# Cross-attention and FP4 FFN on one core: start of the first block, the pair loop of its weight phase, and the softmax between blocks in another order

## Chip, cores and metric

The kernel runs on one NeuronCore of a Trainium2 chip. The metric is device time in microseconds (us). PE is TensorE (matmuls), ACT is ScalarE, DVE is VectorE, POOL is GpSimd, SP is SyncE, which here only issues DMAs.

## What is computed

Two layers on x (2 x 2048 rows of 512): a cross attention over 77 text tokens whose scores are additive, then an FFN whose operands are quantised blockwise to FP4.

```python
f = layernorm(x)                                          # 4096 rows in all, d = 512
h = tanh((ctx @ Ws)[:, None] + (f @ W)[:, :, None] + b)   # per row, per token, per feature
rho = (h @ w) + mask;  att = softmax(rho)                 # 77 scores per row
txt = att @ ctx
x = x + tanh(txt @ Wcw) * f + tanh(txt @ Wcb)
n = layernorm(x)
gate, y = q4(n) @ q4(w_gate).T, q4(n) @ q4(w_up).T        # w_gate, w_up: 1408 x 512
x = x + q4(silu(gate) * y) @ q4(w_down).T                 # q4: blocks of 16 to FP4 and back
```

The tanh over rows x tokens x features is the largest piece: 4096 * 77 * 512 values.

## The kernel before

The 4096 rows are 32 tiles of 128, in four **blocks** of 1024 rows. Of one block the scores are made in 77 **quads** (QPB). A quad is four ACT instructions of 128x1024 (`tanh_quad`, L438: one feature chunk `e`, four tokens), each into one of four places of half of the ring `hring`, and 16 PE matmuls as the profile counts them (`score_quad`, L548) that reduce them with `w` into `rho`. The ring holds two quads: ACT may write quad n when PE has used quad n - 2 (`quad_used`). Engines run their instructions in written order, and all sync is by semaphores, so the order in each engine's program is the schedule.

**Head** (before the first quad). DVE normalises the 8 tiles of block 0 in two halves of 4 (`rows_head`), PE turns them (`turn_head`), ACT copies them out (`copy_head`), PE makes the text projection (L517) and the eight feature projections (`project_head`, chunk e, half hh), DVE copies each into `featT` (L749). Then PE makes `uv` (L532). Only then does it come to `score_quad(0)`.

**Block 0** carries two other loads between its quads. The remaining 24 tiles are normalised and projected as 12 **pairs**: DVE `rows_pair(w)` (L754 to L736), PE `turn_pair(w)` (L563), DVE `copy_pair(w)` (L762), PE `project_pair(w, 0)` and `(w, 1)` (L575), DVE `features_pair(w)` (L773). And DVE quantises the FFN weights: 11 times a piece of gate and one of up (`gate_up_weights`, 128x512 each, L694 to L717), then 4 pieces of down (`down_weights`, 128x1408). One loop on DVE holds both. On PE, pair w is turned after quad `at(w)`, and `project_pair(w - 1, ...)` follows quads `at(w) + 1` and `at(w) + 2`, so behind `turn_pair(w)`.

**FFN tiles.** From tile t = 0 on, each tile has seven steps on PE: `gate_up(t, 0..3)` (L611) and `down(t - 1, 0..2)` (L623). The quads of the next block are spread over these steps by cost in the table `slots`. ACT makes `silu_tanh` (L458) after step 0 to 3's quads plus two; DVE makes `hidden` (L908, L909), `rows_tile(t + 1)` and `quantise_hidden(t)` (L694 to L717 at 128x1408). Scoring of block k ends in step (t, 2) of t = 6, 14, 22 (`SOFTMAX_AT`), and there the **block change** lies: `softmax_drain` (DVE L847, frees `rho`), `softmax_transposes` of two halves (PE L599), `softmax_shift` of two halves (DVE L854, L855), `softmax_exp` (ACT), `softmax_sums` (DVE), `softmax_gates` (ACT), `softmax_factors` (DVE), which tile t + 2 needs.

```python
for w in range(NC + KC):           # DVE, block 0
    ...
    if w < PAIRS:
        copy_pair(w)
    if 0 < w <= PAIRS:
        features_pair(w - 1)
    if w + 1 < PAIRS:
        rows_pair(w + 1)
```

Of the kernel before, what the change touches and what calls it, by code (L numbers as in the profile page):

```python
# [29 lines left out]
def bass_xattn_fp4_ffn(nc, x, ctx_in, mask_in, Ws_in, W_in, w_in, b_in, Wcw_in, bcw_in, Wcb_in, bcb_in,  # L30
# [29 lines left out]
    def quad_at(q):  # L60
        if q < 2 * KC:
            return q % 2, q // 2
        return q // KC, q % KC
# [16 lines left out]
    for k in range(1, NBLK):  # L80
        t0, p0 = (0, 0) if k == 1 else (BASE[k - 1] - 2, 5)
# [25 lines left out]
    with ctx:  # L107
# [6 lines left out]
        def sem(name):  # L114
# [75 lines left out]
                     [rho[:, 0:512], rho[:, 512:1024], tr[:, :], dn[:, :]]]  # L190

# [25 lines left out]
        text_filled = sem("text_filled")  # L217
        bias_ready = sem("bias_ready")
# [31 lines left out]
        FEAT = [(0, 0), (1, 0), (0, 1), (1, 1), (2, 0), (2, 1), (3, 0), (3, 1)]  # L250

        def feat_at(e):
            return max(i for i, (ee, _) in enumerate(FEAT) if ee == e) + 1

# [4 lines left out]
        def _(sp):  # L259
# [8 lines left out]
            sp.dma_start(Wf, W_in.rearrange("(k p) e -> p k e", p=P)).then_inc(loaded_w, 16)  # L268

# [18 lines left out]
            load_gu(1, 0)  # L288
            sp.wait_ge(head_turned, 2)
# [95 lines left out]
        def _(act):  # L385
            act.dma_start(ctx_nat[0:TOK], ctx_in.rearrange("b t d -> t b d")).then_inc(loaded_ctx, 16)
            for n, src in enumerate((w_in, b_in, Wcw_in, Wcb_in)):
                flat = src.rearrange("a b -> (a b)")
                act.dma_start(cols[:, n, :], flat.rearrange("(k p) -> p k", p=P),
                              allow_slow_non_contiguous=True).then_inc(loaded_c, 16)  # L390
            act.dma_start(Wsf, Ws_in.rearrange("(k p) e -> p k e", p=P)).then_inc(loaded_ws, 16)
            for n, src in enumerate((bcw_in, bcb_in)):
                act.dma_start(bc[:, n:n + 1], src.rearrange("(a n) -> a n", a=1).broadcast_to([P, 1])).then_inc(loaded_c, 16)
            act.wait_ge(mask_filled, 1)
            for g in range(GRP):
                act.dma_start(mask_i[SLOTW * g:SLOTW * g + FULLR, :],
                              mask_in[:, 0:GRP * FULLR].rearrange("b (i g) -> i b g", g=GRP)[:, :, g],
                              allow_slow_non_contiguous=True).then_inc(loaded_m, 16)
            act.dma_start(mask_i[FULLR:FULLR + 1, :], mask_in[:, TOK - 1:TOK].rearrange("b t -> t b"),
                          allow_slow_non_contiguous=True).then_inc(loaded_m, 16)  # L400
# [17 lines left out]
            for e in range(KC):  # L418
                act.wait_ge(text_filled, e // 2 + 1)
                act.activation(bias[:, e, :], gu[0][e // 2][:, (e % 2) * BATCH * TOK:(e % 2 + 1) * BATCH * TOK],  # L420
                               ACT.Identity, bias=cols[:, 1, e:e + 1]).then_inc(bias_ready, 1)
            copy_head(1)
            act.wait_ge(bias_ready, KC)

            def tanh_quad(n):
# [5 lines left out]
                if k == 0 and q < 2 * KC and q % 2 == 0:  # L431
                    act.wait_ge(feat_ready, feat_at(q // 2))
# [50 lines left out]
        def _(pe):  # L483
# [16 lines left out]
            def project_head(i):  # L500
                e, hh = FEAT[i]
                pe.wait_ge(xnT_ready, 4 * hh + 4)
                again = [j for j in range(i) if FEAT[j][0] % 2 == e % 2 and FEAT[j][1] == hh]
                if again:
                    pe.wait_ge(feat_ready, again[-1] + 1)
                for k in range(KC):
                    last = pe.matmul(gu[e % 2][hh][:, :], Wf[:, k, e * P:e * P + P], xnT4[hh][:, k, :],
                                     start=(k == 0), stop=(k == KC - 1))
                last.then_inc(feat_filled, 1)

# [3 lines left out]
            for e in range(KC):  # L514
                o = (e % 2) * BATCH * TOK
                for k in range(KC):
                    last = pe.matmul(gu[0][e // 2][:, o:o + BATCH * TOK], Wsf[:, k, e * P:e * P + P], ctxT[:, k, :],  # L517
                                     start=(k == 0), stop=(k == KC - 1))
                if e % 2:
                    last.then_inc(text_filled, 1)  # L520
            pe.wait_ge(loaded_w, 16)
            pe.wait_ge(bias_ready, KC)
            project_head(0)
            project_head(1)
            turn_head(1)
            for i in range(2, len(FEAT)):
                project_head(i)
            pe.wait_ge(wcol_ready, 1)
            for u in range(2):
                o = u * BATCH * TOK  # L530
                for k in range(KC):
                    last = pe.matmul(tr[:, o:o + BATCH * TOK], wcol[:, u, k, :], ctxT[:, k, :],  # L532
                                     start=(k == 0), stop=(k == KC - 1))
            last.then_inc(uv_filled, 1)
# [19 lines left out]
            def turn_pair(p):  # L554

                pe.wait_ge(xn_ready, HEAD_T + 2 * p + 2)
                if p == 0:
                    pe.wait_ge(uv_ready, 1)
                else:
                    pe.wait_ge(pair_copied, p)  # L560
# [416 lines left out]
```

## Time and profile before

| | |
|---|---|
| median of 3 runs | 1740.33 us (1736.83 to 1742.61) |
| profiled execution | 1740.98 us, span 1739.2 us |
| busy share of the span | PE 85%, ACT 77%, DVE 67% |
| ACT busy | 1347.2 us, of it tanh of the quads 1293.0 us |
| mean granted clock of PE | 0.957 |

The span falls in three parts. To 42 us the head runs; to about 1441 us ACT makes tanh (first beside the pairs, then beside the FFN tiles 0 to 22); from there nine more tiles follow in which DVE is busy nearly all the time. The profile marks in brackets how long an engine sat idle before an instruction, and what released it.

### The profile page before, as it was taken

To read this page: it belongs to the slowest core of one execution; us is meant where nothing else is said; L and a number is where in the kernel's file an instruction comes from. 1 tells how busy PE (TensorE), PEld (TensorE's weight loads), DVE (VectorE), ACT (ScalarE), POOL (GpSimd) and SP (SyncE) were. 2 spreads that over 40 slices of the span, in tenths; PEclk is the share of its full clock that TensorE was granted. 3 is DMA by queue.
4 is the path that set the end of the run, shared out by engine and by line. 5 is a ranking of instruction groups with operands and counts; after the bars stand their busy time and mean duration, and the time that the engine had idled before them with its cause. 6 is when DMAs were issued, how large, how long until landed. Compare 5 with 4: busy or idle time off the path is not lost.

```text
span 1739.2 us, 23935 instructions
## 1 busy us (share of the span) xinstructions
PE 1482.2 (85%) x9752; PEld 651.5 (37%) x9752; DVE 1169.9 (67%) x2111; ACT 1347.2 (77%) x1391; POOL 2.7 (0%) x18
## 2 busy tenths in 40 slices
PE   6788888765888899889999999899999998689886
PEld 4234444311333333333333333333333334345442
DVE  4579999864475435467655555676555557999994
ACT  2798898899999999969999999699999992000000
POOL 0000000000000000000000000000000000000000
PEclk9999999888999999999999999999999999899997
DMA  3123332330011111211211111102211111122212
GB/s 129 37 62 75 74 75 63 76 73 15 13 24 35 35 35 24 36 35 16 55 36 36 36 36 35 36 13 59 35 36 36 35 36 36 37 54 62 58 41 51
DMA packets 180754, 77.88 MB, mean 45 GB/s; under 512 B 163851, under 2 KB 163851, under 8 KB 180645
## 3 DMA queue, kind: packets, MB, share of 16 engines
q1 hardware_dynamic: 177392, 74.99, 19.0%
q10 hardware_dynamic: 3253, 1.37, 0.3%
q8 instruction: 76, 1.25, 0.3%
q14 instruction: 33, 0.27, 0.1%
HBM read 27.85 MB, written 8.39 MB: 21 GB/s over the span
## 4 chain that ended last, share of the span: by engine, by line
ACT 56%; DVE 29%; PE 11%; issue 2%; ACTq 1%; DMA 1%; DVEq 0%; SPq 0%
ACT hring L438 54%; DVE work L703 4%; PE rho L548 3%; DVE work L714 2%; DVE work L715 2%; DVE sm L694 2%; ACT th L458 2%; DVE work L909 1%; DVE work L908 1%; DVE sm L697 1%; DVE work L713 1%; DVE work L712 1%; PE dn L623 1%; DVE work L716 1%; DVE work L717 1%
## 5 line engine op out<-in xcount | busy, mean ns | idle before, releaser
L438 ACT ACTIVATE hring<-featT,bias 128x1024 f32<-128x1024 f32 x1232 | 1293.0, 1140 | 80.9 <-PE rho L548 76.2
L548 PE MATMUL rho<-hring,wslide 128*32 128x512 f32 x4928 | 614.9, 623 | 136.7 <-ACT hring L438 136.7
L548 PEld LDWEIGHTS rho<-hring,wslide 128*32 128x32 f32 x4928 | 133.5, 112 | 499.9 <-ACT hring L438 271.7
L623 PE MATMUL dn<-wd_room,turned 128*128 128x512 f16 x1056 | 243.7, 383 | 13.4 <-DMA turned<-work 13.4
L908 DVE SCALAR_TENSOR_TENSOR work<-th,gu1g 128x352 f32<-128x352 f32 x64 | 33.3, 521 | 266.6 <-ACT th L458 265.9
L611 PE MATMUL gu0g<-wg,turned 128*128 128x352 f16 x768 | 134.6, 328 | 45.8 <-DVE work L909 29.0
L623 PEld LDWEIGHTS dn<-wd_room,turned 128*128 128x128 f16 x1056 | 99.2, 98 | 175.2 <-issue 54.6
L458 ACT ACTIVATE th<-gu0g 128x352 f32<-128x352 f32 x64 | 28.9, 451 | 171.5 <-PE gu0u L611 171.5
L611 PE MATMUL gu0u<-wu,turned 128*128 128x352 f16 x768 | 127.5, 317 | 0.0
L611 PE MATMUL gu1g<-wg,turned 128*128 128x352 f16 x768 | 126.2, 314 | 0.0
L611 PE MATMUL gu1u<-wu,turned 128*128 128x352 f16 x768 | 125.0, 313 | 0.0
L611 PEld LDWEIGHTS gu0g<-wg,turned 128*128 128x128 f16 x768 | 73.4, 101 | 127.6 <-issue 35.8
L908 DVE SCALAR_TENSOR_TENSOR work<-th,gu0g 128x352 f32<-128x352 f32 x64 | 33.3, 521 | 120.1 <-ACT th L458 117.9
L611 PEld LDWEIGHTS gu1g<-wg,turned 128*128 128x128 f16 x768 | 71.6, 98 | 74.6 <-issue 39.4
L703 DVE TENSOR_TENSOR work<-work,sm 128x1408 f32<-128x1408 f32 x34 | 93.9, 2762 | 1.2
L611 PEld LDWEIGHTS gu0u<-wu,turned 128*128 128x128 f16 x768 | 76.3, 99 | 41.9
L611 PEld LDWEIGHTS gu1u<-wu,turned 128*128 128x128 f16 x768 | 75.1, 98 | 39.5
L458 ACT ACTIVATE th<-gu1g 128x352 f32<-128x352 f32 x64 | 29.0, 454 | 68.1 <-PE gu1u L611 68.1
L714 DVE TENSOR_TENSOR work<-work 128x1408 f32<-128x1408 f32 (+1 forms) x56 | 70.5, 1259 | 1.9
L715 DVE TENSOR_TENSOR work<-work 128x1408 f16<-128x1408 f32 (+1 forms) x56 | 70.5, 1258 | 1.9
L694 DVE TENSOR_REDUCE sm<-work 128x88 f32<-128x1408 f32 x34 | 55.1, 1620 | 1.2
L697 DVE RECIPROCAL sm<-sm 128x88 f32<-128x88 f32 (+1 forms) x90 | 44.3, 493 | 3.1
(147 smaller groups left out, 1077.5 us busy)
## 6 DMA issues: line engine op xcount, KB each, us to landing
xt<-in_x SPq DMA_DIRECT2D x32, 256.0 KB, 2.8
out<-xt SPq DMA_DIRECT2D x32, 256.0 KB, 2.3
work<-in_x SPq DMA_DIRECT2D x10, 512.0 KB, 4.4
xt<-in_x SPq DMA_DIRECT2D x6, 512.0 KB, 3.9
xt<-in_L_ffn_w_gate SPq DMA_DIRECT2D x11, 256.0 KB, 2.6
xt<-in_L_ffn_w_up SPq DMA_DIRECT2D x11, 256.0 KB, 3.4
work<-in_L_ffn_w_down SPq DMA_DIRECT2D x2, 704.0 KB, 4.6
xt<-in_L_ffn_w_down SPq DMA_DIRECT2D x2, 704.0 KB, 4.6
```

The lines of the kernel that those rows point to most:

```text
L438: act.activation(hring[:, s // 2, g, (s % 2) * 512:(s % 2) * 512 + rows], featT[:, e, ROW0[k]:ROW0[k] + rows], ACT.Tanh, bias=bias[:, e, b ...
L458: act.activation(th[:, n % 2, :], gu[n % 2][0][:, 0:GU_N], ACT.Tanh, scale=0.5 / W_PRE).then_inc(th_ready, 1)
L548: last = pe.matmul(rho[SLOTW * g:SLOTW * g + SLOTW, hf * 512:hf * 512 + 512], wslide[:, e, SLOTW - 1 - r:2 * SLOTW - 1 - r], hring[:, s // ...
L611: last = pe.matmul(ps[:, 0:GU_N], xqT[:, a, k, :], w[:, bb, k, n * GU_N:n * GU_N + GU_N], start=(k == 0 and i == 0), stop=(k == KC - 1 and ...
L623: last = pe.matmul(dn[:, :], hqT[:, a, c, :], wd[:, bb, c, :], start=(c == 0 and i == 0), stop=(c == NC - 1 and i == 2))
L694: step(dve.tensor_reduce(am, v, axis=AX_X, op=ALU.max, apply_absolute_value=True))
L697: step(dve.reciprocal(r, s))
L703: ins = tt(a.rearrange("p (i q b) -> p i b q", **natural), src.rearrange("p (i b q) -> p i b q", **natural), r.rearrange("p (i b) -> p i b ...
L712: step(ts(m.bitcast(I32), a.bitcast(I32), 0x7F800000, None, ALU.bitwise_and))
L714: step(tt(a, a, m, ALU.add))
L715: step(tt(q, a, m, ALU.subtract))
L908: step(stt(h, th[:, n % 2, :], 1.0, gu[n % 2][0][:, 0:GU_N], ALU.add, ALU.mult))
```

## The change

1. **Head.** The first 16 quads go chunk by chunk (four quads for e = 0, four for e = 1, ...) instead of alternating e = 0 and 1. PE projects text and features of chunk 0 only, and one half of chunk 1, and starts scoring; the rest stands between quads 0 to 7. ACT keeps only the bias of chunk 0; DVE makes the others (`text_bias`). Eleven small DMAs (w, b, Wcw, Wcb, bcw, bcb, five of the mask) move from ACT's queue to SP's, behind the x tiles and W.
2. **Pairs.** `turn_pair(w)` follows quad 9 + 5w (before: 5 + 4.5w). In DVE's loop `features_pair(w - 1)` now stands between the two quantisations of a round.
3. **Block changes.** Drain and first shift stand ahead of `hidden(t, 3)`, the second shift right behind it, all ahead of `quantise_hidden(t)`; both transposes stand in step (t, 3), around the first quad of the new block; new quads start in step 3 instead of 5; `softmax_exp` one step sooner on ACT.

```diff
     def quad_at(q):
-        if q < 2 * KC:
-            return q % 2, q // 2
+        if q < KC * KC:
+            return q % KC, q // KC
...
-        t0, p0 = (0, 0) if k == 1 else (BASE[k - 1] - 2, 5)
+        t0, p0 = (0, 0) if k == 1 else (BASE[k - 1] - 2, 3)
...
+        feat_bank = [[gu[1][0][:, :], gu[1][1][:, :]], [tr[:, :], dn[:, :]]]
...
+            act.wait_ge(text_filled, 1)
+            act.activation(bias[:, 0, :], text_bank[0], ACT.Identity, bias=cols[:, 1, 0:1]).then_inc(bias0_ready, 1)
             copy_head(1)
-            act.wait_ge(bias_ready, KC)
+            act.wait_ge(bias0_ready, 1)
...
+                    if t - 1 in SOFTMAX_AT and n == 0:
+                        softmax_exp(SOFTMAX_AT[t - 1])
                     silu_tanh(t, n)
-                    if t - 1 in SOFTMAX_AT and n == 1:
-                        softmax_exp(SOFTMAX_AT[t - 1])
...
+            project_text(0)
             pe.wait_ge(loaded_w, 16)
...
+            project_head(0, 0)
             turn_head(1)
...
+            project_head(0, 1)
+            project_text(1)
+            project_head(1, 0)
             pe.wait_ge(slide_ready, 1)
...
             for n in range(QPB):
                 score_quad(n)
+                if n == 0:
+                    project_head(1, 1)
+                if n == 2:
+                    project_text(2)
+                    project_head(2, 0)
+                if n == 3:
+                    project_head(2, 1)
+                if n == 5:
+                    project_text(3)
+                    project_head(3, 0)
+                if n == 6:
+                    project_head(3, 1)
+                if n == 7:
+                    project_uv()
                 for w in range(PAIRS + 1):
-                    at = 5 + (9 * w) // 2
+                    at = 9 + 5 * w
...
-                    if t in SOFTMAX_AT and p == 5:
+                    if t in SOFTMAX_AT and p == 3:
                         softmax_transposes(SOFTMAX_AT[t], 0)
...
                     for n in slots.get((t, p), ()):
                         score_quad(n)
+                    if t in SOFTMAX_AT and p == 3 and halves(SOFTMAX_AT[t]) == 2:
+                        softmax_transposes(SOFTMAX_AT[t], 1)
...
+            def gate_up_pair(w):
+                gate_up_weights(w, 0)
+                if w == 0:
+                    text_bias(2)
+                    features_head(2)
+                elif w <= PAIRS:
+                    features_pair(w - 1)
+                gate_up_weights(w, 1)
...
             for w in range(NC + KC):
                 if w < NC:
-                    gate_up_weights(w)
+                    gate_up_pair(w)
                 else:
                     down_weights(w - NC)
+                    if w <= PAIRS:
+                        features_pair(w - 1)
                 if w < PAIRS:
                     copy_pair(w)
-                if 0 < w <= PAIRS:
-                    features_pair(w - 1)
...
                 hidden(t, 2)
+                if begun is not None:
+                    softmax_drain(begun)
+                    softmax_shift(begun, 0)
                 hidden(t, 3)
+                if begun is not None and halves(begun) == 2:
+                    softmax_shift(begun, 1)
...
-                if begun is not None:
-                    softmax_drain(begun)
                 quantise_hidden(t)
                 if t > 0:
                     result(t - 1)
                 if begun is not None:
-                    softmax_shift(begun, 0)
                     restart()
```

On DVE, in one round of the loop over pairs and weights in the kernel before, the second quantisation ends (`work<-work,s_lo`), the turned pair is copied out (`stage`), the projected pair before it is copied to `featT`, and the next pair begins (`bn`):

```order
L716 TENSOR_TENSOR work<-work,s_hi 128x512
L717 TENSOR_TENSOR work<-work,s_lo 128x512
L762 COPY stage<-tr 128x4x128
L762 COPY stage<-dn 128x4x128
L773 COPY featT<-gu0g 128x2x256
L773 COPY featT<-gu0u 128x2x256
L754 BN_STATS bn<-work 128x6 x2
```

In the changed kernel the same copies to `featT` stand here, behind the first quantisation (`xq`) and ahead of the second:

```order
L735 TENSOR_TENSOR xq<-work,s_hi 128x512
L736 TENSOR_TENSOR xq<-work,s_lo 128x512
L797 COPY featT<-gu0g 128x2x256
L797 COPY featT<-gu0u 128x2x256
L713 TENSOR_REDUCE sm<-xt 128x32
```

They moved ahead by the second quantisation and the copy of the turned pair.

On PE, the stretch from one pair to the next before (`tr`, `dn` are the turned pair, `gu0`, `gu1` the projected one ahead of it; 8 rho matmuls here are one quad):

```order
L563 MATMUL tr<-idf,xt 128x128 x4
L563 MATMUL dn<-idf,xt 128x128 x4
L548 MATMUL rho<-hring,wslide 32x512 x8
L575 MATMUL gu0g<-stage,turned 128x256 x8
L548 MATMUL rho<-hring,wslide 32x512 x8
L575 MATMUL gu0u<-stage,turned 128x256 x8
L548 MATMUL rho<-hring,wslide 32x512 x24
```

and in the changed kernel, whose other distance (x16 before every second pair) is gone:

```order
L568 MATMUL tr<-idf,xt 128x128 x4
L568 MATMUL dn<-idf,xt 128x128 x4
L553 MATMUL rho<-hring,wslide 32x512 x8
L580 MATMUL gu0g<-stage,turned 128x256 x8
L553 MATMUL rho<-hring,wslide 32x512 x8
L580 MATMUL gu0u<-stage,turned 128x256 x8
L553 MATMUL rho<-hring,wslide 32x512 x24
```

The order within a pair is the same: the projection still stands behind the turning of the next pair.

At a block change (`tr<-gat` is a softmax transpose) PE had, from the last gate step of tile 14 on:

```order
L611 MATMUL gu1g<-wg,turned 128x352 x12
L611 MATMUL gu1u<-wu,turned 128x352 x12
L623 MATMUL dn<-wd_room,turned 128x512 x24
L599 MATMUL tr<-gat,stage 128x128 x4
L548 MATMUL rho<-hring,wslide 32x512 x8
L623 MATMUL dn<-wd_room,turned 128x512 x9
L548 MATMUL rho<-hring,wslide 32x512 x8
L611 MATMUL gu0g<-wg,turned 128x352 x12
L611 MATMUL gu0u<-wu,turned 128x352 x12
L599 MATMUL tr<-gat,stage 128x128 x4
L548 MATMUL rho<-hring,wslide 32x512 x8
```

and has now:

```order
L630 MATMUL gu1g<-wg,turned 128x352 x12
L630 MATMUL gu1u<-wu,turned 128x352 x12
L618 MATMUL tr<-gat,stage 128x128 x4
L553 MATMUL rho<-hring,wslide 32x512 x8
L618 MATMUL tr<-gat,stage 128x128 x4
L642 MATMUL dn<-wd_room,turned 128x512 x12
L553 MATMUL rho<-hring,wslide 32x512 x8
L642 MATMUL dn<-wd_room,turned 128x512 x12
L553 MATMUL rho<-hring,wslide 32x512 x8
L642 MATMUL dn<-wd_room,turned 128x512 x9
```

Both transposes now precede the down steps, and a quad stands behind each down step.

## Rows read from the trace of the kernel before

**Rows 1.** The costliest group: busy, mean ns of one, idle before, releaser

```profile
L438 ACT ACTIVATE hring<-featT,bias 128x1024 f32<-128x1024 f32 x1232 | 1293.0, 1140 | 80.9 <-PE rho L548 76.2
```

**Rows 2.** Timeline, ACT, 0 to 64: start, duration, what, [idle before <- releaser]

```profile
18.27 1.28 ACT L405 ACT_TABLE_LOAD   x1 [18.27 <-issue]
...
42.15 8.42 ACT L438 ACTIVATE hring<-featT,bias 128x1024 f32<-128x1024 f32 x8 [4.64 <-DVE featT L749]
62.45 2.19 ACT L438 ACTIVATE hring<-featT,bias 128x1024 f32<-128x1024 f32 x2 [11.88 <-PE rho L548]
```

**Rows 3.** Timeline, all engines, head

```profile
20.82 2.29 DVE L736 TENSOR_SCALAR work<-work,stat,rstd 128x512 f32<-128x512 f32 x4
...
31.37 3.60 PE L507 MATMUL gu1g<-stage,turned 128*128 128x512 f32 x8
```

**Rows 4.** Windows, 9 to 12: busy time per engine, PE clock, DMA share, GB/s

```profile
9.00:12.00 3.00, 0.00 (x0) 0.00 (x0) 2.48 (x16) 0.00 (x0) 0.00 (x0) 1.00 1.10 364
```

**Rows 5.** Timeline, DVE, one round of the pair loop

```profile
183.41 0.69 DVE L694 TENSOR_REDUCE sm<-xt 128x32 f32<-128x512 f32 x1
...
196.71 0.69 DVE L762 COPY stage<-tr 128x512 f32<-128x512 f32 x1
...
198.21 0.69 DVE L773 COPY featT<-gu0g 128x512 f32<-128x512 f32 x1
...
199.66 1.42 DVE L754 BATCH_NORM_STATS2 bn<-work 128x6 f32<-128x512 f32 x2
...
205.09 0.69 DVE L694 TENSOR_REDUCE sm<-xt 128x32 f32<-128x512 f32 x1
```

**Rows 6.** Timeline, PE, a quad; turns and second projections of three pairs

```profile
105.89 1.93 PE L548 MATMUL rho<-hring,wslide 128*32 128x512 f32 x16
107.74 3.72 PE L575 MATMUL gu0u<-stage,turned 128*128 128x256 f32 x16
...
120.93 0.66 PE L563 MATMUL tr<-idf,work 128*128 128x128 f32 x4
...
129.31 3.72 PE L575 MATMUL gu1u<-stage,turned 128*128 128x256 f32 x16
...
183.44 1.11 PE L563 MATMUL tr<-idf,xt 128*128 128x128 f32 x4 [4.53 <-DVE xt L736]
...
194.38 3.72 PE L575 MATMUL gu0u<-stage,turned 128*128 128x256 f32 x16
...
313.32 1.12 PE L563 MATMUL tr<-idf,xt 128*128 128x128 f32 x4 [4.20 <-DVE xt L736]
```

**Rows 7.** Timeline, DVE, end of block 0

```profile
390.39 0.06 DVE L671 MEMSET marker<- 128x1 f32 x1 [5.41 <-DMA wd_room<-work]
410.85 1.28 DVE L847 TENSOR_SCALAR stage<-rho,negm 128x1024 f32<-128x1024 f32 x1 [20.40 <-PE rho L548]
```

**Rows 8.** Timeline, ACT, first block change, and one row of the second

```profile
755.87 8.42 ACT L438 ACTIVATE hring<-featT,bias 128x1024 f32<-128x1024 f32 x8 [5.63 <-PE rho L548]
...
773.50 4.27 ACT L438 ACTIVATE hring<-featT,bias 128x1024 f32<-128x1024 f32 x4 [8.87 <-PE rho L548]
...
818.68 4.27 ACT L438 ACTIVATE hring<-featT,bias 128x1024 f32<-128x1024 f32 x4 [0.63 <-PE rho L548]
...
824.23 8.43 ACT L438 ACTIVATE hring<-featT,bias 128x1024 f32<-128x1024 f32 x8 [0.93 <-PE rho L548]
...
1123.91 4.27 ACT L438 ACTIVATE hring<-featT,bias 128x1024 f32<-128x1024 f32 x4 [9.67 <-PE rho L548]
```

**Rows 9.** Timeline, PE, first block change: last gate step, two down steps

```profile
743.13 1.96 PE L611 MATMUL gu1g<-wg,turned 128*128 128x352 f16 x12
...
746.72 5.34 PE L623 MATMUL dn<-wd_room,turned 128*128 128x512 f16 x24
```

**Rows 10.** Timeline, DVE, third block change: idle ahead of hidden and shift

```profile
1447.59 0.52 DVE L908 SCALAR_TENSOR_TENSOR work<-th,gu1g 128x352 f32<-128x352 f32 x1 [4.55 <-ACT th L458]
...
1467.96 0.69 DVE L854 TENSOR_REDUCE mx<-tr 128x4 f32<-128x512 f32 x1 [0.97 <-PE tr L599]
...
1472.56 0.52 DVE L908 SCALAR_TENSOR_TENSOR work<-th,gu1g 128x352 f32<-128x352 f32 x1 [3.18 <-ACT th L458]
```

More of the change, by code:

```diff
@@ L248, in bass_xattn_fp4_ffn @@
         down_free = sem("down_free")
-        FEAT = [(0, 0), (1, 0), (0, 1), (1, 1), (2, 0), (2, 1), (3, 0), (3, 1)]
-        def feat_at(e):
-            return max(i for i, (ee, _) in enumerate(FEAT) if ee == e) + 1
+        FEAT = [(e, hh) for e in range(KC) for hh in range(2)]
         block = ctx.enter_context(nc.Block())
@@ L498, in turn_head, with project_head, project_text, project_uv @@
                     last.then_inc(head_turned, 1)
-            def project_head(i):
-                e, hh = FEAT[i]
+            def project_head(e, hh):
                 pe.wait_ge(xnT_ready, 4 * hh + 4)
-                again = [j for j in range(i) if FEAT[j][0] % 2 == e % 2 and FEAT[j][1] == hh]
-                if again:
-                    pe.wait_ge(feat_ready, again[-1] + 1)
+                if e >= 2:
+                    pe.wait_ge(feat_ready, 2 * (e - 2) + hh + 1)
                 for k in range(KC):
-                    last = pe.matmul(gu[e % 2][hh][:, :], Wf[:, k, e * P:e * P + P], xnT4[hh][:, k, :],
+                    last = pe.matmul(feat_bank[e % 2][hh], Wf[:, k, e * P:e * P + P], xnT4[hh][:, k, :],
                                      start=(k == 0), stop=(k == KC - 1))
                 last.then_inc(feat_filled, 1)
+            def project_text(e):
+                if e == 2:
+                    pe.wait_ge(bias0_ready, 1)
+                if e == 3:
+                    pe.wait_ge(bias_ready, 1)
+                for k in range(KC):
+                    last = pe.matmul(text_bank[e], Wsf[:, k, e * P:e * P + P], ctxT[:, k, :],
+                                     start=(k == 0), stop=(k == KC - 1))
+                last.then_inc(text_filled, 1)
+            def project_uv():
+                pe.wait_ge(wcol_ready, 1)
+                pe.wait_ge(bias_ready, 2)
+                for u in range(2):
+                    for k in range(KC):
+                        last = pe.matmul(uv_bank[:, u * BATCH * TOK:(u + 1) * BATCH * TOK], wcol[:, u, k, :],
+                                         ctxT[:, k, :], start=(k == 0), stop=(k == KC - 1))
+                last.then_inc(uv_filled, 1)
             turn_head(0)
@@ L810, in _ @@
                     signal(ins, wcol_ready, 1)
-            for i in range(len(FEAT)):
-                features_head(i)
-            dve.wait_ge(uv_filled, 1)
-            tok_uv = tr[:, 0:2 * BATCH * TOK].rearrange("p (u b t) -> p b u t", u=2, b=BATCH)
-            step(dve.tensor_copy(uv[:, :, :, FULLR:FULLR + 1], tok_uv[:, :, :, TOK - 1:TOK]))
-            for bt in range(BATCH):
-                for u in range(2):
-                    ins = dve.tensor_copy(
-                        uv[:, bt, u, :].rearrange("p (g i) -> p i g", g=GRP)[:, 0:FULLR, :],
-                        tok_uv[:, bt, u, 0:GRP * FULLR].rearrange("p (i g) -> p i g", g=GRP))
-                    if bt == BATCH - 1 and u == 1:
-                        signal(ins, uv_ready, 1)
-                    else:
-                        step(ins)
+            features_head(0)
+            text_bias(1)
+            rows_pair(0)
+            features_head(1)
             dve.wait_ge(loaded_m, 16 * (GRP + 1))
@@ L933, in _ @@
                 hidden(t, 0)
-                if ending is not None and halves(ending) == 2:
-                    softmax_shift(ending, 1)
                 hidden(t, 1)
```

108 lines of the change are left out of this document (54 added, 54 removed).

## Prediction

> **What bounds the kernel now.** I read the costliest group first: ACT's tanh is busy 1293.0 us of the span and idle only 80.9 before it, nearly all of that for PE to free the ring [rows 1]. So what delays a quad on PE delays the end. Next, ACT's timeline, for where those stops are: 11.88 us behind the first two quads [rows 2], small ones all through the pair phase, and four at each of two block changes [rows 8]. Then, for the pair phase, the other two engines. DVE's round from one pair to the next takes 205.09 - 183.41 = 21.7 us without a pause [rows 5], and PE sits 4.53 us and 4.20 us before turning a pair, released by DVE [rows 6]. So from the third pair on DVE sets the pace of block 0, although its share of the span is only 67%. Behind the last quad (tiles 23 to 31) DVE is the bound again; its only long pauses there lie at the third block change [rows 10].
>
> I write X(w) for the start of `turn_pair(w)` on PE, F(w) for the end of `project_pair(w - 1, 1)` behind it.
>
> **1. Head: gain 25 us at quad 14.** ACT came free at 18.27 [rows 2], behind its DMA issues. With two issues left it is free before it is needed, and DVE's normalising sets the pace: the last row of the second half ends at 20.82 + 2.29 = 23.1 [rows 3]. From there: transposes 0.5, ACT copy 0.7, projection of chunk 0's second half 3.5 (3.43 to 3.60 per eight [rows 3]), DVE copy 0.7 (as the 0.69 copies in [rows 5]), handovers 0.3: first tanh at 28.8 instead of 42.15. All issues of the eleven moved DMAs now queue on SP ahead of weights and pairs; the first reader of a pair is DVE at about 29, of the columns ACT's bias at 18, so I see them hidden; if the columns came after 23.1, start would slip by as much.
>
> One thing can hold the x rows themselves: Ws, 1 MB, is issued behind one transfer instead of five, and the DMA engines are full there, at 364 GB/s [rows 4]; 1 MB is 2.9 us at that rate. Bounds are 28.8 (Ws costs x nothing) and 31.7 (all of it ahead of x); I take 29.5, near the lower, because the small transfers that ran there before go away. The Trainium skill ("DMA: Bandwidth & Descriptors", Queues, rings and completion order) says that each DMA engine takes turns between the queues that have work, packet by packet; by that Ws takes half of the rate beside x, and the start would be nearer to 31.
>
> From the start to quad 14 used: 15 quads of 4 x 1.04 = 4.16 us (8.42 us for eight instructions [rows 2]) = 62.4, two stops of about 1.1 where a projection of 3.5 stands between quads (a quad takes PE 1.85, from 105.89 to 107.74 [rows 6]; with a projection of 3.5 ahead of it PE frees a place of the ring after 5.4 where ACT wants it after 4.2), and 1.9 for the last quad: X(1) = 29.5 + 66.6 = 96.1. Before, the quad 14 was used at about 120.9, where pair 2 is turned [rows 6].
>
> **2. Pair loop: loss, and the largest term.** Before, DVE does, after `rows_pair(w)`: two quantisations 13.3, copy 1.5, and then meets `features_pair(w - 1)` at 198.21, which PE ended at 194.38 + 3.72 = 198.1 [rows 5, 6]. X(w) was 183.44, right behind `rows_pair(w)`. So PE needs F - X = 14.7 us, DVE has 14.8 us of other work: the latency is just covered. Moved ahead of the second quantisation and the copy, it has 6.65 us of cover. PE's order is unchanged, the projection still stands behind `turn_pair(w)`, and that behind `rows_pair(w)`. So each round becomes a closed ring of waits:
> X(w) -> F (PE) -> `features_pair` 1.45 -> second quantisation 6.65 -> `copy_pair` 1.45 -> `rows_pair(w + 1)` 205.09 - 199.66 = 5.43 -> X(w + 1). With 0.1 of handover that is 15.1 + (F - X).
> F - X: 12.1 where PE had not stood (120.93 to 129.31 + 3.72), 14.7 after a stop of 4.53 [rows 6]; the other pairs lie between. After the longer stops PE's first matmuls run at about half rate (1.11 for four transposes against 0.66). In the new loop PE is done with the pair's quads 22 us after X and then stands 7 us, longer than any stop here. I take 14.3, near that end, so a round is 29.4; ends are 12.1 + 15.1 = 27.2 and 29.8. ACT needs 5 x 4.16 = 20.8 for the five quads of a round, so it stands 8.6 us per round.
> X(2) = 96.1 + 12.6 + 15.1 = 123.8 (only short stops ahead of it). X(11) = 123.8 + 9 x 29.4 = 388.4, against 313.32 [rows 6].
>
> **3. End of block 0.** Behind X(11) the order is as before: `down_weights` four times, each with its turning DMA, DVE free at 390.39, 77.1 us after X(11) [rows 6, 7]. Then it waited 20.40 us for quad 76; this slack goes. Now quad 76 is 12 quads behind X(11), about 52 us, so DVE is later by 25 us: drain(0) at 388.4 + 77.1 = 465.5, against 410.85 [rows 7]. **+54.7 us** at the drain (head gain and slack already in it). Everything behind it, FFN included, shifts.
>
> **4. Two block changes inside the tanh stream.** Stepped from PE's last gate step at 743.13 [rows 9]. Drain 743.2 to 744.5 (1.28 [rows 7]); gate step to 746.9; first transposes to 748.0; quad 154 to 749.9; shift 0 to 749.4; transposes to 750.9; `hidden` (its tanh at 750.2) and shift 1 to 752.9. ACT goes on at 750.2: the stop of 5.63 is gone. The quads behind the down steps (2.7 each, half of 5.34 [rows 9]) end at 755.5 and 760.0, ACT needs them at 754.4 and 759.7: stops 1.1 and 0.3. The stop of 8.87 is gone, since no transposes wait for `quantise_hidden`. Behind `quantise_hidden`, two `hidden` and `softmax_sums` (unchanged in themselves) DVE is at 788.1, ACT stands 1.0 at the gates; x of tile 8 is turned 3.6 us sooner, and one stop of 0.6 stays. Sum 3.0 after, against 5.63 + 8.87 + 0.63 + 0.93 = 16.1; at the second change 9.67 stands for 8.87 (the other three within 0.01): 16.9. **-13.0 and -13.8.** `quantise_hidden` starts 0.2 us later; cover is gone only if PE's steps slip by 2.3 us (4.16 - 1.85), then ACT stops for the rest. The new slots give each tile 9.6 quads instead of 9.9; PE needs 9.6 x 1.85, four gate steps of 3.7 and 7.2 of down = 39.8 against ACT's 9.6 x 4.16 + 1.4 = 41.3, so I cost the spread at nothing, bounds 0 and +3.
>
> **5. Third block change.** DVE-bound: pauses 4.55 + 0.97 + 3.18 = 8.7 [rows 10]. After: 3.6, by the steps of 4: the drain is done 1.4 after the last quad, the first transposes, behind a gate step, at 4.8. That and 0.2 of handovers make 3.6; the rest has work. 8.7 - 3.6 = 5.1, taken as **-5.0**.
>
> **Sum.** 1740.98 (profiled execution; the median 1740.33 is 0.65 lower) + 54.7 - 26.8 - 5.0 = **1763.9 us**, rounded 1764.
>
> **Rivals.**
> A. The forecast, ring of waits at half-rate restarts. 1764, own range 1752 to 1772: nine rounds 0.4 longer are +4, start +2; rounds of 28.5 are -8, start and changes -4. Chance 0.80.
> B. The ring closes, but PE restarts at full rate. F - X 12.1, X(11) = 96.1 + 10 x 27.2 = 368.1, 20.3 less: 1743.6, within 0.3%. For it: 120.93 [rows 6]. Against: the rows behind stops. Chance 0.08.
> C. Faster: the copy isn't waited for, and the loop stays at 21.7. X(11) = 96.1 + 217 = 313, drain at 390 instead of 410.85, -21; with -31.8: 1688. It decides from F - X below 11.6 on: the nine rounds must lose 24 us, 2.6 each. It needs PE to come to the projection ahead of DVE's rows; the order of rows on PE speaks against. Chance 0.05. The Trainium skill ("Perfetto Trace Analysis", Identifying the Most-Contended Engine) takes the ScalarE or VectorE with the highest occupancy as the one to relieve, here ACT; by it this case would hold, as the change takes ACT stops away everywhere else. The trace disagrees in the pair phase, where DVE at 67% overall paces ACT.
> D. The change doesn't do what it says at the block changes: the shift moves the stop to another place (gates, x). The 31.8 stay out: 1795. Against: the steps of 4 leave more than 1 us at each hand-over. Chance 0.05.
> The rest, 0.02, is unnamed.
>
> **Numbers.** What can be told from no change is 0.3%, 5 us. Range: A's own, from 1751 for the half of the way to B, to 1772; B, C, D and a little of A's tails, under 0.2, are out. Faster 0.06 (C), same 0.08 (B), slower 0.86 (A, D).
>
> **What would show it.** First tanh at 29 to 31; quad 14 near 96. In DVE's waits a new line of about 7 us, ten times, ahead of the `featT` copies of pairs, released by PE; none before it. PE's turns 29 us apart, ACT's tanh in groups of five quads with 8 us between. Drain(0) with no wait ahead of it, at 460 to 470. ACT's stops at 750 and 1100 (shifted) of 1 us. Wrong if the turns are 21 to 23 us apart, if the first tanh is after 35 (columns late on SP's queue), or if ACT still stands 5 us or more behind a block change.

## The result

| | before | after |
|---|---|---|
| median, runs side by side | 1738.74 us (1736.83 to 1742.61, 4 runs) | 1768.49 us (1765.94 to 1771.41, 4 runs) |
| profiled execution, span | 1740.98, 1739.2 us | 1767.55, 1765.7 us |
| PE, ACT, DVE busy | 85%, 77%, 67% | 84%, 76%, 66% |
| mean granted clock of PE | 0.957 | 0.947 |

The ratio is 1.0163, 95% interval 1.0143 to 1.0182: 30 us slower. Forecast were 1764 us, range 1751 to 1772.

The profile's page of the kernel after, its costliest group; it answers to [rows 1]:

```profile
L440 ACT ACTIVATE hring<-featT,bias 128x1024 f32<-128x1024 f32 x1232 | 1295.4, 1148 | 97.7 <-PE rho L553 92.2
```

The tanh itself is the same (1295.4 against 1293.0); its idle time grew by 17 us. What else there is, the waits of the kernel after show (columns: engine, line, for whom; us in total, times, longest):

```profile
ACT hring L440 <- PE rho L553: 92.2, 43, 6.2
...
DVE featT L797 <- PE gu0u L580: 51.9, 6, 19.9
DVE featT L797 <- PE gu1u L580: 44.8, 6, 8.5
...
ACT stage L448 <- DVE stage L895: 29.9, 4, 21.7
```

ACT now also stands 21.7 us ahead of the exponentials of block 0, which is booked on another line than tanh. And DVE waits 96.7 us, in twelve portions, ahead of the copy of a pair to `featT`; in the kernel before it waited there twice, 5.9 and 5.5 us, and not in the round of [rows 5]. The longest portion, 19.9 us, is that of pair 0, before the pair loop is in its rhythm; the nine of pairs 1 to 9 are 6.9 to 8.5 us each, 69 us in all; pairs 10 and 11 have 1.7 and 5.9. The nine are, as experiments 1 and 4 bear out, the cause of the other two waits; where they come from is seen in DVE's and PE's timelines.

One round of the pair loop in the timeline of DVE, kernel after (start, duration, what, [idle before <- releaser]), from one copy to `featT` to the next:

```profile
140.03 0.69 DVE L797 COPY featT<-gu1g 128x512 f32<-128x512 f32 x1 [7.21 <-PE gu1u L580]
...
148.12 0.69 DVE L786 COPY stage<-tr 128x512 f32<-128x512 f32 x1
...
155.00 0.69 DVE L713 TENSOR_REDUCE sm<-xt 128x32 f32<-128x512 f32 x1
...
169.78 0.69 DVE L797 COPY featT<-gu0g 128x512 f32<-128x512 f32 x1 [8.17 <-PE gu0u L580]
```

The same round on PE, kernel after:

```profile
126.24 1.11 PE L568 MATMUL tr<-idf,work 128*128 128x128 f32 x4 [6.93 <-DVE work L755]
...
155.02 1.11 PE L568 MATMUL tr<-idf,xt 128*128 128x128 f32 x4 [5.66 <-DVE xt L755]
...
156.91 3.60 PE L553 MATMUL rho<-hring,wslide 128*32 128x512 f32 x16
160.44 3.72 PE L580 MATMUL gu0g<-stage,turned 128*128 128x256 f32 x16
...
165.95 3.72 PE L580 MATMUL gu0u<-stage,turned 128*128 128x256 f32 x16
...
184.76 1.12 PE L568 MATMUL tr<-idf,work 128*128 128x128 f32 x4 [6.92 <-DVE work L755]
```

Follow the releasers: DVE ends `rows_pair` at 155.0, PE turns at 155.02 and ends the projection of the pair before at 165.95 + 3.72 = 169.67, DVE copies at 169.78, quantises, copies the turned pair, makes the next rows, and PE turns at 184.76. Each waits for the other once in a round; nobody's own work sets the 29.7 us. In between ACT fills both halves of `hring` and stands: 6.16 + 1.23 + 1.24 = 8.6 us in this round.

The turns are at 99.04 (pair 1), 126.24, 155.02, 184.76, 213.29, 242.92, 273.04, 301.81, 331.54, 360.07 and 389.69 (pair 11): (389.69 - 126.24) / 9 = 29.27 us a round, against 21.7 [rows 5].

End of block 0, timeline of DVE, kernel after; it answers to [rows 7]:

```profile
467.14 0.06 DVE L690 MEMSET marker<- 128x1 f32 x1 [5.38 <-DMA wd_room<-work]
467.36 1.28 DVE L887 TENSOR_SCALAR stage<-rho,negm 128x1024 f32<-128x1024 f32 x1 [0.15 <-DVE marker L690]
```

The 20.40 us that DVE waited for quad 76 are gone: DVE comes last, and the drain is at 467.36 instead of 410.85. The quads start again 59.15 us later than before; ACT's rows of this place, first the kernel before, then after:

```profile
418.45 8.41 ACT L438 ACTIVATE hring<-featT,bias 128x1024 f32<-128x1024 f32 x8
```

```profile
472.40 0.63 ACT L448 ACTIVATE stage<-stage 128x512 f32<-128x512 f32 x1 [21.75 <-DVE stage L895]
...
477.60 8.40 ACT L440 ACTIVATE hring<-featT,bias 128x1024 f32<-128x1024 f32 x8
```

From there the change gives time back. First block change, timeline of ACT, kernel after, against [rows 8]:

```profile
813.58 4.27 ACT L440 ACTIVATE hring<-featT,bias 128x1024 f32<-128x1024 f32 x4 [0.84 <-PE rho L553]
818.13 8.42 ACT L440 ACTIVATE hring<-featT,bias 128x1024 f32<-128x1024 f32 x8 [0.28 <-PE rho L553]
...
846.25 0.49 ACT L454 ACTIVATE gates<-garg,bc 128x8 f32<-128x8 f32 x2 [0.98 <-DVE garg L909]
...
873.02 7.39 ACT L440 ACTIVATE hring<-featT,bias 128x1024 f32<-128x1024 f32 x7 [0.64 <-PE rho L553]
```

The stops are 0.84 + 0.28 + 0.98 + 0.64 = 2.7 us instead of 16.1; at the second change (0.84, 0.28, 1.00, 0.65) 2.8 instead of 16.9. At the third change DVE's pauses are 4.1 us instead of 8.7, against [rows 10]:

```profile
1474.93 1.28 DVE L887 TENSOR_SCALAR stage<-rho,negm 128x1024 f32<-128x1024 f32 x1 [0.53 <-PE rho L553]
1479.48 0.69 DVE L894 TENSOR_REDUCE mx<-tr 128x4 f32<-128x512 f32 x1 [3.27 <-PE tr L618]
...
1482.28 0.69 DVE L894 TENSOR_REDUCE mx<-tr 128x4 f32<-128x512 f32 x1 [0.28 <-PE tr L618]
```

The balance, place by place: +59.15 where block 1's quads start; behind the last quad, at the first silu tanh of tile 22 (1441.23 before, 1472.72 after), +31.5, so the two changes gave 27.7; at the end of the span (1739.2, 1765.7) +26.5, so the third gave 5.0. The medians differ by 29.8, that is 3.3 us more; the runs of one kernel scatter by some 5 us.

### The profile page after: what moved, and what is told of

It reads as the page before. It is cut to its first block, busy times and chain, and to the rows that moved or that the text cites. A ratio compares the mean times of both kernels' runs of the same rounds, so it can differ in the third digit from the quotient of the medians.

```text
span 1765.7 us, 23940 instructions
## 1 busy us (share of the span) xinstructions
PE 1481.3 (84%) x9752; PEld 650.8 (37%) x9752; DVE 1171.3 (66%) x2114; ACT 1348.3 (76%) x1388; POOL 2.7 (0%) x18
## 4 chain that ended last, share of the span: by engine, by line
ACT 44%; DVE 28%; PE 25%; DMA 2%; issue 2%; DVEq 0%; SPq 0%; ACTq 0%
ACT hring L440 42%; PE rho L553 9%; PE dn L642 3%; DVE work L722 3%; DVE work L733 2%; DVE work L734 2%; DVE sm L713 2%; PE gu1g L580 1%; ACT th L460 1%; PE gu0g L580 1%; PE gu1u L580 1%; PE gu0u L580 1%; PE gu1g L630 1%; PE gu0g L630 1%; DVE work L948 1%
## 5 line engine op out<-in xcount | busy, mean ns | idle before, releaser
L440 ACT ACTIVATE hring<-featT,bias 128x1024 f32<-128x1024 f32 x1232 | 1295.4, 1148 | 97.7 <-PE rho L553 92.2
L642 PE MATMUL dn<-wd_room,turned 128*128 128x512 f16 x1056 | 243.1, 382 | 13.4 <-DMA turned<-work 13.4
L460 ACT ACTIVATE th<-gu0g 128x352 f32<-128x352 f32 x64 | 29.3, 458 | 173.1 <-PE gu0u L630 173.1
L460 ACT ACTIVATE th<-gu1g 128x352 f32<-128x352 f32 x64 | 29.4, 459 | 58.3 <-PE gu1u L630 58.3
```

The lines of the kernel that those rows point to most:

```text
L440: act.activation(hring[:, s // 2, g, (s % 2) * 512:(s % 2) * 512 + rows], featT[:, e, ROW0[k]:ROW0[k] + rows], ACT.Tanh, bias=bias[:, e, b ...
L460: act.activation(th[:, n % 2, :], gu[n % 2][0][:, 0:GU_N], ACT.Tanh, scale=0.5 / W_PRE).then_inc(th_ready, 1)
L642: last = pe.matmul(dn[:, :], hqT[:, a, c, :], wd[:, bb, c, :], start=(c == 0 and i == 0), stop=(c == NC - 1 and i == 2))
```

## Experiments

Two theories stood at the start. **Ring of waits:** the move of one copy (1.45 us of DVE) ahead of the second quantisation turned a covered latency into a closed ring of waits, and that alone costs the time. **Spacing:** the pairs come later on PE (9 + 5w), and everything behind them slides. Ratios are to the kernel before, run on the same chip between these.

**1. The copy back to its place.** The changed kernel, all else kept:

```diff
                 elif w <= PAIRS:
-                    features_pair(w - 1)
                 gate_up_weights(w, 1)
...
                 if w < PAIRS:
                     copy_pair(w)
+                if 0 < w <= PAIRS:
+                    features_pair(w - 1)
```

> The changed kernel with features_pair(w - 1) put back behind copy_pair(w); all else stays, the spacing of 9 + 5w too. Ring of waits (the copy ahead of the second quantisation has only 6.65 us of cover for a latency of 13 to 15): the round falls from 29.3 to DVE's own 21.7 us, pair 11 is turned at about 316 instead of 389.7, the drain of block 0 at about 393 instead of 467.4, so about 74 us less: 1694 us, 44 less than the kernel before. Spacing theory (pairs lie half a quad further apart and start four quads later, so DVE ends later): the spacing stays, so about 1768 us, turns still 29 us apart.

Measured 1688.81 us, before 1741.25; ratio 0.9705 (0.9690 to 0.9719). The spacing is the changed one and the loss is gone: some 80 us between this kernel and the changed one hang on one position of a copy. (Places can be compared in the profiled executions alone, and this kernel's took 1693.37 us, longer than its median: 77.3 us less where block 1's quads start, 74.1 at the end of the span, near the 74 expected.) Rounds are (315.46 - 120.70) / 9 = 21.6 us, and of its waits, shown as above, this is what is left:

```profile
ACT hring L440 <- PE rho L553: 19.2, 25, 1.2
...
ACT stage L448 <- DVE stage L893: 29.8, 4, 21.7
```

Its second line shows that DVE still ends block 0 (drain at 390.17), which experiment 8 takes up.

**2. The copy alone moved.** The kernel before with `features_pair(w - 1)` between the two quantisations, nothing else:

```diff
                 for m in range(2):
+                    if m == 1 and i > 0:
+                        features_pair(i - 1)
...
-                if 0 < w <= PAIRS:
+                if NC <= w <= PAIRS:
                     features_pair(w - 1)
```

> The kernel before with one edit: features_pair(w - 1) stands between the two quantisations of a round. Ring of waits: pair 2 is turned at 98.75 + 12.6 + 15.1 = 126.5, then nine rounds of 29.3, pair 11 at about 390 instead of 313.3, drain at 467 instead of 410.85, and about 2.6 us more as the softmax transposes start from a cold PE: 1798 us (+59). Spacing theory: the spacing is the old one, so nothing is lost: within 5 us of 1739.

1818.92 us; 1.0449 (1.0433 to 1.0464). Rounds are 29.3 here too, (390.25 - 126.44) / 9, so the ring does not need the new spacing. But the loss is 78 us where I had expected 57. The drain, timeline of DVE in this kernel, shows why:

```profile
467.78 0.06 DVE L671 MEMSET marker<- 128x1 f32 x1 [5.42 <-DMA wd_room<-work]
487.61 1.28 DVE L849 TENSOR_SCALAR stage<-rho,negm 128x1024 f32<-128x1024 f32 x1 [19.77 <-PE rho L548]
```

DVE is ready at 467.8, about where my sum had it, but quad 76 comes 20 us later. With 5 + 4.5w pair 11 is turned after quad 54, and 22 quads are left (97 us, from 390.25 to 487.61); with 9 + 5w it is turned after quad 64, and 12 are left. My expectation had taken the drain for the changed kernel's. That explanation was then tested:

**3. The same with even spacing.**

```diff
-                    at = 5 + (9 * w) // 2
+                    at = 5 + 5 * w
```

> The kernel before with the copy to featT between the quantisations (as in the run that gave 1818.9 us), and the pairs turned after quad 5 + 5w instead of 5 + 4.5w. Theory (what comes after the ring of waits depends on how many quads are left behind the last turn): rounds stay 29.1, X(11) near 390, but 60 instead of 54 quads are used by then, so that the drain is set by DVE at X(11) + 77 = 467 instead of by quad 76 at 487: 1796 to 1801 us. Rival (the 20 us that this kernel took beyond my expectation have another cause, in the block changes or in the ring itself): 1815 to 1820 us.

1805.26 us, before 1739.87; 1.0376 (1.0357 to 1.0394). Between the two, nearer to the theory: DVE no longer waits ahead of the drain, which is at 471.70, not 467, since pair 1 is turned a quad later than in the run above (102.06 against 99.06) and pair 11 at 394.03. So of the 20 us in excess 16 are gone at the drain, 14.7 at the next tanh (496.59 and 481.94, of which the first is 9.0 us behind its drain and the second 10.2), 12 in the medians (77.7 and 65.4 above before). The new spacing hides part of what the moved copy costs.

**4. PE's order instead of DVE's.** The changed kernel, its copy left between the quantisations, but PE projects pair w - 1 ahead of turning pair w:

```diff
-                    if n == at and w < PAIRS:
-                        turn_pair(w)
-                    if n == at + 1 and w > 0:
+                    if n == at - 2 and w > 0:
                         project_pair(w - 1, 0)
-                    if n == at + 2 and w > 0:
+                    if n == at - 1 and w > 0:
                         project_pair(w - 1, 1)
+                    if n == at and w < PAIRS:
+                        turn_pair(w)
```

> The changed kernel with the copy left between the quantisations, but project_pair(w - 1) on PE ahead of turn_pair(w) (behind quads 9 + 5w - 2 and - 1). Ring of waits: what closes the ring is that the projection stands behind a turning that needs DVE's next rows; with the order on PE reversed the projection needs only copy_pair(w - 1), one round old, and DVE no longer waits 7 us per round. Turns 21 to 23 us apart, drain at about 390 to 397, 1690 to 1698 us. If instead the place of the copy on DVE alone were at fault (whatever PE does): about 1768 us.

1691.03 us; 0.9710 (0.9694 to 0.9726), against 1688.81 in experiment 1. The early copy costs next to nothing when the projection does not stand behind a turn that waits for DVE. So it is neither the copy's place as such nor contention of DVE with PE: it is the edge from `rows_pair(w)` over `turn_pair(w)` to the projection of w - 1 that closes the ring. Turns are (322.86 - 99.84) / 10 = 22.3 apart, which is about ACT's five quads (20.8) and its short stops of 0.6 to 1.2 beside the projections; none waits for DVE any more, and the drain is at 390.33. Timeline of PE in this kernel:

```profile
160.41 3.72 PE L580 MATMUL gu1u<-stage,turned 128*128 128x256 f32 x16
...
165.92 0.66 PE L568 MATMUL tr<-idf,work 128*128 128x128 f32 x4
```

**5. A longer ring.** The changed kernel with the copy ahead of both quantisations, to see whether a round is the sum of its members:

```diff
             def gate_up_pair(w):
+                if 0 < w <= PAIRS:
+                    features_pair(w - 1)
                 gate_up_weights(w, 0)
                 if w == 0:
                     text_bias(2)
                     features_head(2)
-                elif w <= PAIRS:
-                    features_pair(w - 1)
```

> The changed kernel with the copy of the projected pair to featT ahead of both quantisations instead of between them, so that DVE has no other work between rows_pair(w) and the copy. Ring of waits: a round is the sum of its members, (F - X) + copy 1.45 + both quantisations 13.3 + copy of the turned pair 1.45 + rows_pair 5.43 + 0.1 = 21.7 + (F - X). With PE standing still longer ahead of each turn, F - X is 13.6 to 14.7: rounds of 35.3 to 36.4 where they were 29.3, ten of them, 60 to 71 us on the drain, 1829 to 1840 us. Rival (what the wait costs does not depend on how much work stands between rows and copy, for instance DVE slowed as such while PE projects): rounds stay near 29.3, 1768 us.

1832.90 us; 1.0536 (1.0521 to 1.0552). Turns at 132.81 (pair 2) and 455.26 (pair 11): 35.8 a round, which is 21.7 + 14.1, and F - X is 13.6 to 14.8 in the trace. 6.65 us more in the ring of waits made the round 6.6 longer.

**6. The other member, F - X.** The changed kernel with ten matmuls of no use (their results are not read) in PE's idle time ahead of the turns of pairs 2 to 11:

```diff
             def turn_pair(p):
+                if p > 1:
+                    pe.wait_ge(pair_copied, p)
+                    for j in range(10):
+                        pe.matmul(tr[:, 0:256], idf[:], xnT2[(p - 1) % 2][:, j % KC, :], start=True, stop=True)
                 pe.wait_ge(xn_ready, HEAD_T + 2 * p + 2)
```

> The changed kernel with ten matmuls on PE, whose results nobody reads, ahead of each turn of pairs 2 to 11 (into tr, before the wait for the rows), some 4.6 us of the 5.4 to 6.9 us that PE stands there. Nothing else changes. Theory (F - X is long because PE restarts at the lower clock after standing): F - X falls from 13.4 to 14.7 to about 12.1 to 12.6, rounds from 29.3 to 27.2 to 27.8, X(11) and the drain 15 to 21 us sooner, 1748 to 1753 us. Rival (F - X is long for another reason, for instance that PE waits for the weights' DMAs or shares something with DVE): rounds stay at 29.3, 1766 to 1771 us, or more where the added matmuls come late.

1749.84 us, before 1739.87; 1.0059 (1.0041 to 1.0077), 20 us less than the changed kernel by the differences to before (10.0 and 29.8). Timeline of PE in this kernel, one round:

```profile
180.29 0.66 PE L572 MATMUL tr<-idf,work 128*128 128x128 f32 x4 [0.85 <-DVE work L759]
...
181.31 1.92 PE L553 MATMUL rho<-hring,wslide 128*32 128x512 f32 x16
...
188.67 3.72 PE L584 MATMUL gu1u<-stage,turned 128*128 128x256 f32 x16
...
202.05 4.58 PE L564 MATMUL tr<-stage,idf 128*128 128x256 f32 x20 [1.49 <-DVE stage L790]
207.48 0.66 PE L572 MATMUL tr<-idf,xt 128*128 128x128 f32 x4 [0.85 <-DVE xt L759]
```

F - X is 188.67 + 3.72 - 180.29 = 12.10 and the round 27.19, the 12.1 + 15.1 of the prediction's lower end, where the changed kernel has 14.65 and 29.74 in the round above. The granted clock says the same. Two windows of the kernel after (the figure ahead of the last two is the clock): the turn and the first quad, then the 15.5 us behind them:

```profile
155.02:160.44 5.42, 5.42 (x24) 2.16 (x24) 5.04 (x12) 0.00 (x0) 0.00 (x0) 0.51 0.16 46
160.44:175.91 15.47, 12.80 (x84) 7.27 (x81) 6.82 (x16) 12.85 (x13) 0.00 (x0) 1.00 0.22 55
```

So behind the 5.66 us of standing PE runs at the lower of its two levels (1.2 GHz) through the transposes and a quad, then at 2.4 GHz. In the run with the added matmuls the turn and the first quad (180.29 to 183.17) have clock 1.00. What the ten restarts cost, 19 to 20 us, is 1.1% of the span. The Trainium skill ("TensorE: Matmul & The Clock Gate", What's actually happening) puts the ramp, for modelling, at under 1% of a typical kernel span. Here it comes to a little more, since a restart lies inside the ring of waits and is paid in each round.

**7. Block changes alone.** The kernel before with part 3 of the change and nothing of parts 1 and 2; the core of the edit:

```diff
-        t0, p0 = (0, 0) if k == 1 else (BASE[k - 1] - 2, 5)
+        t0, p0 = (0, 0) if k == 1 else (BASE[k - 1] - 2, 3)
...
-                    if t in SOFTMAX_AT and p == 5:
+                    if t in SOFTMAX_AT and p == 3:
                         softmax_transposes(SOFTMAX_AT[t], 0)
...
                 hidden(t, 2)
+                if begun is not None:
+                    softmax_drain(begun)
+                    softmax_shift(begun, 0)
                 hidden(t, 3)
+                if begun is not None and halves(begun) == 2:
+                    softmax_shift(begun, 1)
```

> The kernel before with the part on block changes alone (head and pair loop as before). By the sum: stops of ACT of 16.1 and 16.9 us shrink to 2.8 each, and DVE's 8.7 us at the third change to 3.6: 32.5 us less, 1706 us. If the gain at the changes were given back behind them (x of the next tile late, PE too full for the new slots): less than half of that, above 1722 us.

1708.51 us; 0.9814 (0.9799 to 0.9828): -32.7 us by the medians. The first change in ACT's timeline of this kernel:

```profile
756.61 4.27 ACT L438 ACTIVATE hring<-featT,bias 128x1024 f32<-128x1024 f32 x4 [0.84 <-PE rho L548]
...
789.28 0.49 ACT L452 ACTIVATE gates<-garg,bc 128x8 f32<-128x8 f32 x2 [0.99 <-DVE garg L869]
...
816.06 8.43 ACT L438 ACTIVATE hring<-featT,bias 128x1024 f32<-128x1024 f32 x8 [0.65 <-PE rho L548]
```

The parts add up: experiment 1 has this and the head and spacing, and is 19.7 us below, which is what the head and the spacing bring with an open ring (tanh of block 1 starts at 400.35 there, at 419.80 here). No run has the head or the spacing alone, so how the 19.7 us divide between them is not shown.

**8. A better version.** In experiment 1 DVE ended block 0, and it stood 9.6 us ahead of its first copy to `featT` (111.13) and 5.3 ahead of its last (350.80). (The expectation below takes the 5.3 for a pause ahead of the second copy; there it is 0.15.) Pair 0 can be turned sooner. The kernel of experiment 1 with

```diff
-                    at = 9 + 5 * w
+                    at = 8 + (9 * w) // 2
```

> The changed kernel with the copy to featT behind the quantisations (as in the run that gave 1688.8 us) and, besides, pair w turned after quad 8 + 4.5w instead of 9 + 5w. In that run DVE still ended block 0: drain at 390.17 with ACT standing about 22 us for it, DVE's rounds 21.7 us without a pause, but two pauses of 9.6 and 5.3 us ahead of its first two copies of pairs. Theory (DVE sets the end of block 0, its start late by those pauses): turning pair 0 one quad and pair 1 two quads sooner takes 4 to 8 us off each of the next pauses, the drain comes 8 to 10 us sooner, 1679 to 1682 us. Rival (ACT's quads or the ring set it, or the pauses only move): 1686 to 1690 us.

1685.23 us, before 1739.87; 0.9688 (0.9674 to 0.9703): between the two. DVE came 8 us sooner (ready at 381.78 instead of 389.96), as many as the theory had, though not where it had them: 4.3 are the first pause (5.31 instead of 9.61) and 4.3 shorter waits for the first two turned pairs, while the pause ahead of the last copy is 5.9. But then it waited:

```profile
381.78 0.06 DVE L690 MEMSET marker<- 128x1 f32 x1 [5.37 <-DMA wd_room<-work]
388.09 1.28 DVE L885 TENSOR_SCALAR stage<-rho,negm 128x1024 f32<-128x1024 f32 x1 [6.25 <-PE rho L553]
```

As in experiment 2, a closer spacing leaves more quads behind the last turn. The drain needs two things, DVE and quad 76, and I had looked at one. A spacing between the two, `at = 8 + (14 * w) // 3`:

> The changed kernel with the copy to featT behind the quantisations and pair w turned after quad 8 + 14w/3 (rounded down), so after quads 8, 12, 17, ... 59. In the run with 8 + 4.5w DVE was ready for the drain at 381.8 but waited 6.25 us for quad 76 (used at 388), in the one with 9 + 5w it was DVE that came last, at 390. Theory (the drain is the later of DVE and quad 76): two quads fewer behind the last turn bring quad 76 to about 380, DVE stays at 382, drain at 382 to 383, tanh starts again 7.6 to 10.2 us later, at 390 to 393 instead of 395.7: 1679 to 1683 us. Rival (DVE's rounds grow again when pairs come later on PE): 1685 us or more.

1678.61 us (1678.41 to 1679.73, 5 runs), before 1741.69; 0.9640 (0.9621 to 0.9658), some 90 us below the changed kernel. DVE is ready at 380.10 and the drain follows at 380.31 without a wait for quad 76; tanh starts again at 390.11. This is the best kernel of the study.

## Why the prediction was right

Its verdict and its mechanism held; rival A happened, with 1768.5 for 1764. Point by point:

- **Head.** First tanh at 30.07, taken 29.5, bounds 28.8 and 31.7. The rows come one microsecond later, not 2.9: DVE starts the last step of its second half at 21.78 where it was 20.82 [rows 3]. All of it is there at the first pair of tiles (8.58, before 7.63). That Ws beside x is the reason is argued only; no run moves it alone. 30.07 lies between the 29.5 taken and the 31 that equal turns of the two queues would give, and does not decide between them. The columns' DMAs, now late on SP's queue, are waited for once, hidden:

```profile
19.59 0.39 ACT L421 ACTIVATE bias<-gu0g,cols 128x154 f32<-128x154 f32 x1 [1.62 <-DMA bc<-in_L_xattn_bcb]
...
30.07 20.89 ACT L440 ACTIVATE hring<-featT,bias 128x1024 f32<-128x1024 f32 x20 [4.65 <-DVE featT L768]
51.23 4.27 ACT L440 ACTIVATE hring<-featT,bias 128x1024 f32<-128x1024 f32 x4 [0.26 <-PE rho L553]
56.72 12.58 ACT L440 ACTIVATE hring<-featT,bias 128x1024 f32<-128x1024 f32 x12 [1.22 <-PE rho L553]
70.45 41.67 ACT L440 ACTIVATE hring<-featT,bias 128x1024 f32<-128x1024 f32 x40 [1.16 <-PE rho L553]
```

  The stops between the quads are 0.26 + 1.22 + 1.16 = 2.6 (taken 2.2).
- **X(1)** came at 99.04, not 96.1. The last quad ahead of it took PE 3.56 us, not the 1.9 of the sum; with the later start and the stops that is 1.7 + 0.6 + 0.4 of the 2.9. PE's granted clock in that quad is 0.53, with no stop longer than 2.24 us in the 16 us ahead of it; the sum had no restart there.
- **Round.** 29.27, taken 29.4, as 15.1 + F - X; in the round shown above the 15.1 is 15.09. Of the bounds for F - X, 12.1 and 14.7, the lower is right (experiment 6) and the upper a little low: the changed kernel has 13.4 (184.76 to 194.48 + 3.72) to 15.0 (242.92 to 254.22 + 3.72), and that round is 30.1, above the 29.8 of the prediction. X(11) at 389.69, taken 388.4, is nearer than its parts, by luck: X(1) was 2.9 late, the first round 0.5 and the other nine together 1.2 shorter than taken.
- **Drain** at 467.36, taken 465.5; tail 77.7, taken 77.1. DVE last, as predicted. ACT stands 8.6 us per round, as taken, but in three parts (some 5 to 6.2, then twice about 1.2) and not between groups of five quads.
- **Missed:** the sum moved everything behind the drain by the drain's shift, 56.5 as measured. But the quads started 59.15 later, 10.2 us behind the drain instead of 7.6 (410.85 to 418.45). Timeline of PE at the first half of the softmax, kernel before, then after:

```profile
412.28 1.13 PE L599 MATMUL tr<-gat,stage 128*128 128x128 f32 x8 [1.49 <-DVE stage L847]
...
413.34 1.92 PE L548 MATMUL rho<-hring,wslide 128*32 128x512 f32 x16
```

```profile
468.79 2.05 PE L618 MATMUL tr<-gat,stage 128*128 128x128 f32 x8 [23.95 <-DVE stage L887]
...
470.77 3.64 PE L553 MATMUL rho<-hring,wslide 128*32 128x512 f32 x16
```

  Before, PE came to these transposes from quads, now from 24 us of standing. It runs them and the quad that stands ahead of the second half's at the lower clock (granted 0.51 from 468.79 to 474.50; 1.00 before, from 412.28 to 416.00): 0.92 + 1.72 = 2.6 us, which DVE, and then ACT, wait longer. In the first kernel of experiment 8, where quad 76 comes last again, it is 7.6 once more (388.09 to 395.69). But PE at work on quads does not make sure of it: in experiment 2 quad 76 comes last too, PE stands 1.48 us, and the transposes take 2.04, the quad 2.39 and the way to the next tanh 9.0. The step that was mis-sized is "Everything behind it, FFN included, shifts": while DVE waited for quad 76, PE had been making quads, and with that wait gone PE stands.
- **Block changes.** 13.3 and 14.1, taken 13.0 and 13.8; third 5.0 by the span, taken 5.0, though DVE's pauses there are 4.1 where the steps had 3.6. The stepped stops were 1.1, 0.3, 1.0 and 0.6, measured 0.84, 0.28, 0.98 and 0.64. The 3.6 us by which the profiled execution is above the sum are +4.5 at the start of block 1 and -0.9 at the changes. Rival A's upper end of 1772 is 2 us more than 1764 and the two terms named for it.
- **Rivals.** B asked for restarts at full rate. The rows show half rate, and experiment 6 shows what B would have given: 1749.84, not within 0.3%, since its estimate also had the start, X(1) and the cold transposes too low. C is what experiment 1 is: 1688.81 for the 1688 of the sum, but only with DVE's order of before. D is refuted by experiment 7. What I did not see in advance is how much the size of the ring's cost depends on the quads left behind X(11) (experiments 2 and 3).

## What to carry to other kernels

Before a consumer is moved ahead in an in-order program, add up what lies between the producer's trigger and the consumer on both engines: here DVE had 14.8 us of work against 14.7 us of latency, so moving it past 8.1 us of that work cost 7.6 us in every round, although the copy itself takes 1.45. If such a wait closes a ring, its period is the sum of the members, whoever is busiest by share; break it by moving the consumer back (experiment 1, 1688.8 us) or on the engine that runs the producer (experiment 4, 1691.0), which gave nearly the same here. And a point where two streams meet (the drain) is set by the later one: move one only as far as the other lets it.

## What the runs showed of the hardware

- PE's restarts at 1.2 GHz cost time where they lay inside the ring of waits: ten added matmuls per round changed PE's busy time from 182.6 of 263.5 us (granted clock 0.85) to 205.3 of 244.7 us (0.97) over pairs 2 to 11, of it 41 us the added matmuls, and took 19 us off that stretch. In the open order of experiment 1 the rounds are 21.6 us although four transposes take 1.11 us in some turns (at 163.22) and 0.66 in others (at 185.67).
- The lower level does not need a long stop. Ahead of X(1) PE does a quad every 4.15 us and stands 2.23 us between; the same 16 matmuls take 1.92, then 3.03, then 3.56 us, at a granted clock of 1.00 (87.24 to 91.40), 0.58 (to 95.55) and 0.53 (to 99.11), timeline of PE, kernel after:

```profile
87.24 1.92 PE L553 MATMUL rho<-hring,wslide 128*32 128x512 f32 x16 [2.23 <-ACT hring L440]
91.40 3.03 PE L553 MATMUL rho<-hring,wslide 128*32 128x512 f32 x16 [2.24 <-ACT hring L440]
95.55 3.56 PE L553 MATMUL rho<-hring,wslide 128*32 128x512 f32 x16 [1.12 <-ACT hring L440]
```

- With the 1 MB load of Ws issued sooner beside the x rows, and eleven small loads moved behind them, the x rows took 7.2 us from issue to landing (median of the five up to 30 us) instead of 6.3, while the DMA engines moved 386 GB/s from 9 to 12 us (364 before [rows 4]). Which of the two moves makes the difference is not shown.
